# Macaron stack on one core: the deep stage with its norms on VectorE and ScalarE, the softmax multiply on GpSimd, and maxima over an axis in place of a clamp and two copies

## The reference

```
x = attn(shift_tokens(x)) + x
x = ffn(shift_tokens(x)) + x

shift_tokens: the upper half of the channels comes from the token before
attn: qkv = x @ Wqkv                                  # 16 heads of 64
      q = q / max(norm(q), 1e-12) * q_scale            # per head, k the same
      q = q * cos * scale + rotate_half(q) * sin * scale
      k = k * cos / scale + rotate_half(k) * sin / scale
      softmax over a window of 32 keys before and 32 own keys, 8 * q.k
      out = (softmax @ v) @ Wo
ffn:  xn = (x - mean) / sqrt(var + 1e-5) * g + b
      out = a * gelu(gate) @ W2 + b2                   # hidden width 341
```

## Time and profile before

| | us |
|---|---|
| median of the runs | 4751.29 |
| lowest and highest of 3 | 4750.31, 4755.04 |
| the profiled execution, its own time | 4761.42 |
| span of its trace | 4759.7 |
| first deep call, first memset of its pads to its last residual | about 1165 to 2910 |
| second deep call, to the end of the program | about 2994 to 4759 |

### The profile page before, as it was taken

One profiled execution on the slowest core, in us unless ns is written; L12 is line 12 of the kernel. 1 busy time (PEld: TensorE's weight loads), 2 busy tenths in 40 slices (PEclk: granted clock), 3 DMA queues, 4 the chain that ended last, 5 costly groups with the idle time before them and its releaser, 6 DMA issues.

```text
span 4759.7 us, 145988 instructions
## 1 busy us (share of the span) xinstructions
PE 4342.8 (91%) x66028; PEld 2488.3 (52%) x66028; DVE 3414.1 (72%) x3983; ACT 2192.3 (46%) x2409; POOL 3080.7 (65%) x1726
## 2 busy tenths in 40 slices
PE   7999899986899999999999996799999999999998
PEld 3444443343555555555555553455555555555554
DVE  5465656555778778877778875677777777877874
ACT  1242234431455555555555552355545545545553
POOL 0010000011999898889889980799888888988884
PEclk8699889987999999999999997899999999999999
DMA  2000000000111211111111111011111111111111
GB/s 78 1 1 1 0 1 1 1 0 24 28 31 31 56 27 54 32 31 52 30 54 31 31 33 51 18 32 31 54 29 31 54 28 54 31 51 31 30 29 31
DMA packets 78536, 144.58 MB, mean 30 GB/s; under 512 B 18776, under 2 KB 24992, under 8 KB 76384
## 3 DMA queue, kind: packets, MB, share of 16 engines
q1 hardware_dynamic: 77920, 135.23, 11.0%
HBM read 39.75 MB, written 1.05 MB: 9 GB/s over the span
## 4 chain that ended last, share of the span: by engine, by line
PE 57%; POOL 26%; issue 9%; DVE 7%; ACT 1%; DMA 0%; SPq 0%; POOLq 0%; DVEq 0%
POOL arena L1701 9%; PE psum L1288 8%; POOL arena L1694 7%; POOL arena L1707 6%; PE psum L682 5%; PE psum L1319 5%; PE psum L1305 4%; PE psum L1357 4%; PE psum L1257 3%; PE psum L1338 3%; PE psum L1403 3%; PE psum L1352 3%; PE psum L725 2%; POOL rstd L1712 2%; PE psum L708 2%
## 5 line engine op out<-in xcount | busy, mean ns | idle before, releaser
L1701 POOL TENSOR_TENSOR arena<-arena,minus_half 128x16 f32<-128x16 f32 x384 | 1133.0, 2951 | 32.0
L1694 POOL TENSOR_TENSOR arena<-arena 128x1024 f32<-128x1024 f32 x384 | 907.0, 2362 | 16.9 <-DVE arena L1579 16.9
L1575 DVE TENSOR_TENSOR arena<-psum,arena 128x1024 f32<-128x1024 f32 x384 | 467.9, 1218 | 412.1 <-ACT arena L1457 412.1
L1707 POOL TENSOR_TENSOR arena<-arena 128x1024 f32<-128x1024 f32 x384 | 733.7, 1911 | 42.6
L1463 ACT ACTIVATE arena<-psum 128x1024 f32<-128x1024 f32 x384 | 392.2, 1021 | 293.3 <-PE psum L1305 293.3
L1457 ACT ACTIVATE arena<-psum 128x1024 f32<-128x1024 f32 x384 | 391.9, 1021 | 257.1 <-PE psum L1288 252.6
L1579 DVE TENSOR_TENSOR arena<-psum,arena 128x1024 f32<-128x1024 f32 x384 | 466.5, 1215 | 48.6 <-PE psum L1305 47.7
L1305 PEld LDWEIGHTS psum<-w_ident,arena 128*128 128x128 f32 x3072 | 353.0, 141 | 283.1 <-POOL arena L1707 144.7
L1490 ACT ACTIVATE arena<-psum 128x1024 f32<-128x1024 f32 x192 | 196.5, 1024 | 596.4 <-PE psum L1319 596.4
L1338 PE MATMUL psum<-arena 64*64 64x32 f32 x24576 | 416.7, 221 | 55.1 <-issue 55.0
L1586 DVE TENSOR_REDUCE arena<-arena 128x16 f32<-128x1024 f32 x384 | 464.8, 1210 | 2.8
(11 more groups left out here) (270 smaller groups left out, 7300.4 us busy)
## 6 DMA issues: line engine op xcount, KB each, us to landing
arena<-arena SPq DMA_DIRECT2D x672, 128.0 KB
deep_wqkv<-in_deep_wqkv SPq DMA_DIRECT2D x6, 1536.0 KB, 7.4
arena<-in_deep_wqkv SPq DMA_DIRECT2D x6, 1536.0 KB, 7.4
arena<-arena SPq DMA_DIRECT2D x96, 64.0 KB
deep_wo<-in_deep_wo SPq DMA_DIRECT2D x6, 512.0 KB, 7.4
arena<-in_deep_wo SPq DMA_DIRECT2D x6, 512.0 KB, 7.4
deep_w<-in_deep_w SPq DMA_DIRECT2D x6, 341.0 KB, 7.6
arena<-in_deep_w SPq DMA_DIRECT2D x6, 341.0 KB, 7.5
```

Source lines behind the costliest of these rows:

```text
L1575: nc.vector.tensor_tensor(turned[:, hs, :].rearrange("p h (a e) -> p h a e", a=2), swapped, sin, ALU.mult).then_inc(de.deep_rope_parts, 1)
L1694: nc.gpsimd.tensor_tensor(roped[:, hs, :], roped[:, hs, :], turned[:, hs, :], ALU.add).then_inc(de.deep_summed, 1)
L1701: nc.gpsimd.tensor_tensor(h_inv[a % 2][:, hs], h_inv[a % 2][:, hs], minus_half[:, :], ALU.pow).then_inc(de.deep_inv_ready, 1)
L1707: nc.gpsimd.tensor_tensor(roped[:, hs, :], roped[:, hs, :], over(h_inv[a % 2][:, hs], [P, LHEADS, LD]), ALU.mult).then_inc(de.deep_roped, 1)
```

## The change

**Norms.** The sums of squares of both halves go to column 0 of a new tile `h_pair`, whose column 1 holds 1e-24 from the program's start. Once a tile, `norms_dve` takes the maximum over that axis of two (128x32 from 128x64), and the reciprocal; `norms_act` takes the square root on ACT, one step later. `rope_inv_pool` is gone. Before, POOL did the clamp and the power per half.

**Probabilities.** `divide_dve` becomes `divide_pool`, the same multiplication on POOL.

**Copies.** The four shifted copies of a unit (`attn_dve`, `shift_dve`) become `tensor_reduce` with a maximum over an axis of length one.

**Buffers.** `roped` is doubled, `qT` becomes two buffers of one tile. POOL scales tile `s-1` at the start of step `s` instead of tile `s` within it.

**Order.** PE issues the scores and values first, the scores in two parts around `value_pe` (32 small matmuls each) and the mix in two parts around the second `turn_pe`; the mean moves from t = 0 to t = 3, `centre_dve` to the start of the next step, `shift_dve` from t = 2 to t = 1. `spread_pe` is marked as a transpose.

```diff
+        h_pair = sb("h_pair", [P, 2 * LHEADS, 2])
...
-        def scores_pe(pe, c, j):
+        def scores_open_pe(pe, c, j):
...
+            scores_pe(j, 0)
+        def scores_close_pe(pe, c, j):
+            scores_pe(j, 1).then_inc(de.deep_scores_ready, 1)
...
         def turn_pe(pe, c, a, half):
             pe.wait_ge(de.deep_roped, 2 * i + half + 1)
-            if half == 1 and a >= 1:
+            if half == 1:
+                pe.wait_ge(de.deep_turn_kept, 2 * i + 1)
+            elif a >= 1:
                 pe.wait_ge(de.deep_v_kept, i)
...
+        def norms_act(act, c, a):
+            i = c * ALL + a
+            act.wait_ge(de.deep_sq_inv, i + 1)
+            if a >= 2:
+                act.wait_ge(de.deep_roped, 2 * i - 2)
+            nc.scalar.activation(h_inv[a % 2], h_rcp, ACT.Sqrt).then_inc(de.deep_inv_ready, 1)
...
+        def norms_dve(dve, c, a):
+            i = c * ALL + a
+            dve.wait_ge(de.deep_sq_summed, 2 * i + 2)
+            nc.vector.tensor_reduce(h_low, h_pair[:, :, :], AX.X, ALU.max).then_inc(de.deep_clamped, 1)
+            dve.wait_ge(de.deep_clamped, i + 1)
+            if a >= 1:
+                dve.wait_ge(de.deep_inv_ready, i)
+            nc.vector.reciprocal(h_rcp, h_low).then_inc(de.deep_sq_inv, 1)
...
-            nc.vector.tensor_copy(xf[0:64, :], zu[0:64, :]).then_inc(de.deep_ffn_shifted, 1)
-            nc.vector.tensor_copy(xf[64:P, 1:T], zu[64:P, 0:T - 1]).then_inc(de.deep_ffn_shifted, 1)
+            nc.vector.tensor_reduce(xf[0:64, :], single(zu[0:64, :]), AX.X, ALU.max).then_inc(de.deep_ffn_shifted, 1)
+            nc.vector.tensor_reduce(xf[64:P, 1:T], single(zu[64:P, 0:T - 1]), AX.X, ALU.max).then_inc(de.deep_ffn_shifted, 1)
...
-        def rope_inv_pool(pool, c, a, half):
-            i, hs = c * ALL + a, HALVES[half]
-            pool.wait_ge(de.deep_sq_summed, 2 * i + half + 1)
-            nc.gpsimd.tensor_scalar(h_inv[a % 2][:, hs], h_sum[a % 2][:, hs], NORM_FLOOR, None, ALU.max).then_inc(de.deep_clamped, 1)
-            pool.wait_ge(de.deep_clamped, 2 * i + half + 1)
-            nc.gpsimd.tensor_tensor(h_inv[a % 2][:, hs], h_inv[a % 2][:, hs], minus_half[:, :], ALU.pow).then_inc(de.deep_inv_ready, 1)
...
+        def divide_pool(pool, c, j):
+            i = c * ALL + j
+            pool.wait_ge(de.deep_row_inv, i + 1)
+            nc.gpsimd.tensor_tensor(flat[j % 2], flat[j % 2], over(row_inv, R), ALU.mult).then_inc(de.deep_probs_ready, 1)
```

More of the change, by code:

```diff
@@ L1201, in program @@
         tabs = new(4, TILES, LD)
-        qT = new(PAIRS, T)
+        qT = [new(PAIRS, P) for _ in range(2)]
         kT = new(PAIRS, WIN + T)
@@ L1206, in program @@
         turned = new(2 * LHEADS, LD)
-        roped = new(2 * LHEADS, LD)
+        roped = [new(2 * LHEADS, LD) for _ in range(2)]
         probs = [new(PAIRS, 2, 2 * WIN) for _ in range(2)]
@@ L1212, in program @@
         xs = [new(WIN + T) for _ in range(2)]
-        h_sum, h_inv = [new(2 * LHEADS) for _ in range(2)], [new(2 * LHEADS) for _ in range(2)]
+        h_low, h_rcp = new(2 * LHEADS), new(2 * LHEADS)
+        h_inv = [new(2 * LHEADS) for _ in range(2)]
         row_max, row_sum, row_inv = (new(LHEADS) for _ in range(3))
@@ L1252, in scores_pe @@
                                      stop=False, skip_group_check=True)
-            for pair in range(PAIRS):
+            scores_pe(j, 0)
+        def scores_close_pe(pe, c, j):
+            scores_pe(j, 1).then_inc(de.deep_scores_ready, 1)
+        def scores_pe(j, part):
+            t = j % TILES
+            for pair in range(PAIRS // 2 * part, PAIRS // 2 * (part + 1)):
                 for jj in range(WPT):
@@ L1294, in turn_pe @@
             pe.wait_ge(de.deep_roped, 2 * i + half + 1)
[L1295 removed]
+            if half == 1:
+                pe.wait_ge(de.deep_turn_kept, 2 * i + 1)
+            elif a >= 1:
                 pe.wait_ge(de.deep_v_kept, i)
[L1297 to L1302 removed]
             for m in range(PAIRS):
                 h = LHEADS * half + 2 * m
[L1305 removed]
+                last = nc.tensor.matmul(turns[:, m * P:(m + 1) * P], roped[a % 2][:, h:h + 2, :], w.ident[:, :], start=True, stop=True,
                                         is_transpose=True)
@@ L1330, in mix_pe, with mix_close_pe @@
             apart(pe)
-            for pair in range(0, PAIRS, 2):
+            mix_pe(j, 0)
+        def mix_close_pe(pe, c, j):
+            mix_pe(j, 1).then_inc(de.deep_pv_done, 1)
+        def mix_pe(j, part):
+            t = j % TILES
+            for pair in range(PAIRS // 2 * part, PAIRS // 2 * (part + 1), 2):
                 for jj in range(WPT):
@@ L1340, in mix_pe @@
                                                     probsT[64 * r:64 * r + 64, half, col:col + WIN], start=True, stop=True)
-            last.then_inc(de.deep_pv_done, 1)
+            return last
         WO_FIRST = 3
@@ L1576, in parts_dve @@
                                     ALU.mult).then_inc(de.deep_rope_parts, 1)
-            if a >= 1:
-                dve.wait_ge(de.deep_turned, 2 * i - 1 + half)
-            nc.vector.tensor_tensor(roped[:, hs, :], qk_half, under(tabs[:, 2 * half, t, :], shape),
+            if a >= 2:
+                dve.wait_ge(de.deep_turned, 2 * i - 3 + half)
+            nc.vector.tensor_tensor(roped[a % 2][:, hs, :], qk_half, under(tabs[:, 2 * half, t, :], shape),
                                     ALU.mult).then_inc(de.deep_rope_parts, 1)
@@ L1645, in deep_dve @@
                 ending, begun = 0 <= n - 2 < UNITS, 0 <= n - 1 < UNITS
+                if t == 0 and ending:
+                    centre_dve(dve, c, n - 2)
+                if t == 2 and ending:
+                    hidden_dve(dve, c, n - 2, 1)
                 if t == 3 and ending:
@@ L1674, in deep_dve @@
                 if s < ALL:
+                    parts_dve(dve, c, s, 1)
                     squares_dve(dve, c, s, 1)
-                if t == 3 and begun:
-                    centre_dve(dve, c, n - 1)
+                    norms_dve(dve, c, s)
+                if t == 0 and ending:
+                    scale_dve(dve, c, n - 2)
+                if t == 1 and 2 <= n + 1 < UNITS:
+                    shift_dve(dve, c, n + 1)
                 if t == 1 and ending:
```

120 lines of the change are left out of this document (53 added, 67 removed).

## The result

The changed kernel takes 4640.1 us, median of 4 runs (4628.4 to 4648.1); the kernel before, run beside it, 4753.2 (4750.3 to 4757.7). The ratio is 0.9759, with a 95% interval of 0.9736 to 0.9782: faster by 2.4%. The profiled execution took 4648.1 us with a span of 4646.4 (first to last instruction), 113.3 less than that of before.

A forecast was written before the change was run, and what follows sets the result against it. The prediction took PE's own work to bound a unit once POOL left the chain: steps of 67.7 us plus 1.1 issue, 68.8 against 70.3. Gains of 33 plus 10 us in each of two calls gave 4665 us, range 4595 to 4745.

The forecast's parts named there:

- the likeliest case: Whole kernel: 4665 us, a unit at 68.8 us, own range 4640 to 4700, chance 0.49.
- The bound: Deep calls: POOL then PE carry each unit's chain; relieving POOL gives back only what PE does not need itself.
- The added operations: Multiplication on POOL 1.91 us; on ACT a root of 0.27 per tile, table loads of 1.28, nine a unit instead of two.
- PE's own work: PE's matmuls and turns in a unit, t = 0 to 3: 13.4, 16.25, 17.95 and 17.1, together 64.7 us.
- The issue time: PE's runs of small matmuls: of 2.7 us a unit now, two fifths, 1.1, were taken to stay.
- The rival: Issue time in PE's small matmuls vanishes because the runs are cut: a unit 67.7 us, 4617 us, chance 0.20.
- the rival that kept all the issue time: PE's small matmuls keep all 2.7 us of issue time: a unit 70.4 us, 4735 us, chance 0.19.
- The second call: Gain of 43 us a call, from 70.3 us a unit before, counted for two calls: 86 us.
- The start and tail of the calls: First seven or so steps of each call, without feed-forward: 10 us gained a call; the tail stays.
- The dear table change: On ACT a change of table costs its load's time once again: a unit 73 us, 4861 us, chance 0.05.
- The dear maxima: DVE's maxima in place of copies cost by the result, 3.8 us each: a unit 76.7, 5010 us, chance 0.04.
- The small edits at nothing: Second `roped`, split `qT`, copies at 0.69, earlier `shift_dve` and SP's value moves: no effect on the time.

The follow-up runs named there:

- h_both: Changed kernel with ACT's affine behind the root at t = 1, and POOL's probability multiplication ahead of the next tile's rotation sum: 4586.7 us, ratio 0.9628 to the kernel before.
- k_runs_as_before: h_both with the scores in one run ahead of the values, the mix in one run between the turns of k and of the probabilities: ratio 0.9928.
- f_no_loads: Changed kernel with a square in place of the norms' square root, so the table loads around it go (results differ): 4585.8 us, ratio 0.9638.
- j: h_both with both halves of the scores ahead of the values and both halves of the mix ahead of the turn of k: ratio 0.9835.
- b_split: Kernel before with only its runs of small matmuls cut as in the changed one, norms and multiplication left where they were: 4813.1 us, ratio 1.0101.

## Why the prediction was right

The forecast was 4665 and the time is 4640: within the range and the likeliest case's own (4640 to 4700), at its very edge. Step by step:

- **The bound.** Right in the main. POOL left the chain except for its run at t = 0 and one scale at t = 1 (1.91, the wait that the sum had foreseen there), and the rest of a unit is PE. With the power back on POOL the kernel is slower than the one before (c_pow, 1.0333), so the new order and the second buffers are no gain without the move of the norms. What they are worth with it was not tried: no run keeps the move and takes them back.
- **The added operations.** Right: 1.90 for the multiplication (predicted 1.91), 1.02 for the layernorm's power (1.0, and no longer 2.0), 1.28 for a load and 0.24 for the root (0.27), 0.68 for a maximum (0.69). The path at t = 0 gave 14.56 (14.7), at t = 1 17.60 (17.5), at t = 2 18.62 (18.4), at t = 3 17.51 (17.1).
- **PE's own work.** Too low: 64.7 against 66.9 in h_both. I priced each piece by its length in the order of before. Cutting the runs costs time of its own: the same small matmuls are busy 765.3 us instead of 715.4 in rows 6, 1.0 us a unit. The step t = 3, where nothing is waited for, shows the sum's error undisturbed: 17.51 against the 17.1 of the sum, and with whole runs (k_runs_as_before) it is 17.11. So the cut is 0.4 us in that step, and by the estimate above 1.6 of the 2.2 us a unit that were missing. The waits were smaller than foreseen, 0.66 at t = 0 (14.7 - 13.4 = 1.3 foreseen) and 0.69 at t = 1 (1.25), and the steps came out right all the same.
- **The issue time.** This term failed. I took two fifths, 1.1 us a unit, from bounds of 0 and 2.7, with no row to choose by; it is 0. The rival's mechanism was the true one; its 4617 was missed because a unit takes 68.3 and not 67.7. Issue minus 1.1, steps plus 0.6: 68.3 instead of 68.8. Two errors of opposite sign lie in the forecast, and that they partly cancelled is luck: the same sum with the issue term at its true zero is the rival's 4617, 23 us too fast. What whole runs would have given was measured only in h_both with its two orders: k_runs_as_before has 0.9928 with 88 us of issue time at the small matmuls. That is in the direction of the rival that kept all the issue time (4735), and not a test of its number.
- **The second call.** I took 70.3 us a unit for both calls; in the second the kernel before needs 71.1. That is 15 us of gain that one more row would have shown.
- **The start and tail of the calls.** 15.0 and 8.1 for the 10 predicted each; the tails moved by +4.6 and -7.1, together nearly nothing.
- **The dear table change.** Excluded. In the chain the load starts 0.03 us behind the end of the squaring, the root starts 0.01 us behind the end of its load (2046.04 + 1.28 to 2047.33), and f_no_loads gives no more than 0.88 us at t = 1, less than one load's own length. The drain that the Trainium skill names in "ScalarE: Activation LUTs", section "What ACT_TABLE_LOAD costs", would have to show there; this trace does not agree with it.
- **The dear maxima.** Excluded by L1628 at 0.68.
- **The small edits at nothing.** Right for the copies and the spread; for the spread the reason is the wait behind it, which my own working of t = 0 held although the prediction counted 0.5 us for the transpose: where a step is set by POOL's chain, a saving on PE in it is worth nothing.

What stays open: what PE waits for in long stretches of small matmuls (I take it for the supply of instructions, and no run tested that), and what sets its length. Issue time moves between lines as the order changes (10.8 us at the scores in k, 28.5 in j), so only its sum says something. Why it is larger in the second call of before (46 of the 129 us lie between 1300 and 2800) was not tried either.

## What to carry to other kernels

An edit can be a loss alone and a gain together with another: cutting the runs cost 1.0% while POOL was late, is worth 0.4% or nothing in the changed kernel, and 2.1 to 3.1% in h_both, by where the whole runs stand. So a part is to be tried in the kernel it is meant for. When the bound moves to the next engine, read that engine's waits one by one: each of the two that were left cost about what it lasted, and changing two orders gave half as much again as the whole change. And measure the period in every call or repetition, not in the first.

## What the runs showed of the hardware

- In runs of 128 small matmuls (entries in the trace) PE stands still for no cause that the profile names: 129 us at the two lines in the kernel before, 88 in k_runs_as_before. Runs of 64 with larger work between them have 4 us in h_both, but 20.8 in b_split. The cut costs about 60 us of PE's own time (766.3 against 705.4 us of busy time for the same 49152 entries in h_both and k).
- Waits of up to 2.9 us at the turn of q went with a lower granted clock: 0.96 to 0.98 in c_pow against 1.00 in the changed kernel, and a mean of 671 against 619 ns for the same projection matmul.
- A power on GpSimd takes 1.0 us for 4 elements a partition, 2.93 for 16 and 5.44 for 32; the same result over VectorE's reciprocal (0.35), a table load (1.28) and a root (0.24) takes 1.87 at 32 elements, with one more load to come back, and none of GpSimd's time.
- The 424 table loads of the deep calls took 1.283 us each in the mean of every group, and where the chain shown passes one the next operation starts 0.01 us behind it.
- A copy of 64x512 on VectorE took 0.42 us alone and 1.57 where it began inside a GpSimd operation of 1.90; as a maximum over an axis of one it took 0.62 to 0.68 in the changed kernel.
